# A routed last layer: results scattered to token order inside the block loop

## Chip, cores, metric

The kernel runs on one core of one Trainium2 chip. The metric is the device time of one execution in microseconds.

## What is computed

Sixteen sequences of 256 tokens with 256 features pass through four layers, each with a cross attention and a feed-forward part, added to x through a tanh gate. The change lies in the feed-forward part of the last layer, a mixture of experts (T = 32 tiles of 128 tokens, 32 experts, 4 chosen for each token):

```
logits = flat @ router_w.T + router_bias
scores = softmax(logits); topk_scores, topk_idx = top_k(scores, 4)
topk_scores = topk_scores / clip(topk_scores.sum(), 1e-12)
h = silu(einsum('nd,ehd->neh', flat, gate_w)) * einsum('nd,ehd->neh', flat, up_w)
expert_out = einsum('neh,edh->ned', h, down_w)
sel = take_along_axis(expert_out, topk_idx)          # four rows of 256 for each token
out = (sel * topk_scores).sum(axis=1)
out = out + silu(flat @ sgate_w.T) * (flat @ sup_w.T) @ sdown_w.T
x = x + tanh(g_ffn[3]) * out
```

An expert's hidden width is 128, that of the shared part (the last line but one) 512. All is float32.

## The kernel before

The program is a row of stages, each a block in which five engines run their own instruction lists and meet through semaphores. Stage A (0 to some 2360 us) is the first layer, B the routed part of the second, C all up to the router of the last, D the routed and shared part of the last layer. Everything in D comes from `expert_layer(rd, 128, ..., 0, 1, True)`.

**Cells.** In C, the normed rows of each batch of 256 tokens (tiles `x_e[b % 3]`) are scattered by GpSimd (`scatter_rows`, L1917) into a DRAM tensor `d_cells`. It has a region of 4096 rows for each expert and one more; a row's place is its expert's region plus its rank. Stage A clears the tensor with 66 transfers of 2 MB on SP, five after each batch (L477 to L480). VectorE finds ranks and places in `e_rank` (L2832). The eight scatters of the last batch are the first thing that GpSimd does in D.

**Blocks.** The rows of each expert are cut into blocks of 128; NB = 159 is the fixed number of blocks. A block needs the number of its expert (`block_expert`) and its first cell.

**The order in D.** PE computes the first of eight groups of the shared part: four `shared_in` (L1632, 8 products of 512 columns as the profile counts) and four `shared_out` (L1647), with forty products of the identity between them that nobody reads (L1641 and L1642). Then PE runs the loop over blocks. In round u it transposes the rows of block u+1 (`rows`, L1678), multiplies block u by its gate and up weights (`gate_up`, L1689) and the hidden values of block u-1 by the down weights (`down`, L1701). ScalarE makes silu (L1753), then copies the result of block u-1 out of PSUM (`put_rows`, L1745) and asks for its store to `d_results` in block order (L1747). VectorE copies the transposed rows (L1879) and multiplies the two halves (L1889). GpSimd gathers the rows of block u+4 as soon as buffer u % 4 is free (L1601, an indirect DMA). SP brings the 256 KB of gate and up weights of a block into one of eight buffers (L1569).

**The finish.** After the loop, once all results are stored, GpSimd gathers for each tile of tokens and each of its four choices 128 result rows: 128 indirect DMAs (L1610) into eight buffers, each after the first eight waiting for `added`. VectorE weighs them and adds them to x (`result_add`, L1845), four in each step, between the steps of the shared part of the seven other groups, which PE computes meanwhile; a `shared_add` (L1837) waits until the result adds of earlier tiles are done. SP stores x at the end, batch by batch.

**PSUM.** `ring` has three slots of 1024 columns, `acc` two of 512; a name's slot comes from its place in a written order, and `wait_room`, `wait_full`, `wait_taken` are the waits on them.

## Time and profile before

| | |
|---|---|
| median of 3 runs | 4259.48 us (4255.28 to 4262.33) |
| profiled execution | 4255.14 us |
| its span, first to last instruction | 4253.4 us |
| PE busy | 3971.4 us, 93% |
| VectorE, ScalarE, GpSimd busy | 2250.9, 1746.0, 1066.0 us |
| DMA traffic | 472.83 MB, 111 GB/s over the span |
| layer D | 3759.8 us to the end |
| its loop over blocks | 3791.0 to 4053.8 us |

PE is TensorE's products, PEld its weight loads, DVE VectorE, ACT ScalarE, POOL GpSimd, SP the queue of SyncE. A row of a group gives line, engine, operation, output<-inputs, count, then busy us and mean ns, then the engine's idle time just before, with what ended it. The clock is the share of TensorE's full speed that was granted.

### The profile page before, as it was taken

To read this page: it belongs to the slowest core of one execution; us is meant where nothing else is said; L and a number is where in the kernel's file an instruction comes from. 1 tells how busy PE (TensorE), PEld (TensorE's weight loads), DVE (VectorE), ACT (ScalarE), POOL (GpSimd) and SP (SyncE) were. 2 spreads that over 40 slices of the span, in tenths; PEclk is the share of its full clock that TensorE was granted. 3 is DMA by queue.
4 is the path that set the end of the run, shared out by engine and by line. 5 is a ranking of instruction groups with operands and counts; after the bars stand their busy time and mean duration, and the time that the engine had idled before them with its cause. 6 is when DMAs were issued, how large, how long until landed. Compare 5 with 4: busy or idle time off the path is not lost. (4 is left out here: it accounts for less than half of the span.)

```text
span 4253.4 us, 77426 instructions
## 1 busy us (share of the span) xinstructions
PE 3971.4 (93%) x28880; PEld 2796.9 (66%) x28960; DVE 2250.9 (53%) x6853; ACT 1746.0 (41%) x3685; POOL 1066.0 (25%) x1239
## 2 busy tenths in 40 slices
PE   7999999999999999999998899999998898789987
PEld 4666666666666666666665489976666565468854
DVE  4555665566556555655564521136766665344444
ACT  4445554555455545554542111113544444313310
POOL 2221222122212221222120011111022222245555
PEclk9999999999999999999999999999999898899998
DMA  3003303330333033303310169960212111159934
GB/s 116 2 12 117 116 10 110 117 116 9 110 117 117 11 108 117 117 11 108 115 58 28 75 233 333 334 212 28 66 61 70 60 55 47 43 199 321 322 117 131
DMA packets 285453, 472.83 MB, mean 111 GB/s; under 512 B 23009, under 2 KB 224609, under 8 KB 276513
## 3 DMA queue, kind: packets, MB, share of 16 engines
q1 hardware_dynamic: 227632, 371.88, 25.8%
q0 software_dynamic: 24480, 66.88, 5.1%
q10 hardware_dynamic: 32976, 29.13, 2.0%
q8 instruction: 240, 3.93, 0.4%
q14 instruction: 125, 1.02, 0.1%
HBM read 266.74 MB, written 201.06 MB: 110 GB/s over the span
## 5 line engine op out<-in xcount | busy, mean ns | idle before, releaser
L496 POOL TENSOR_SCALAR a_wide_p<-a_wide_p,a_w_inv 128x512 f32<-128x512 f32 x512 | 356.7, 710 | 1440.3 <-DVE a_w_inv L1164 1440.3
L938 ACT ACTIVATE a_wide_p<-a_wide_p,a_row_min 128x512 f32<-128x512 f32 x512 | 363.6, 713 | 120.5 <-DVE a_row_min L1159 120.3
L1234 DVE TENSOR_REDUCE a_q_pad<-ring 128x4 f32<-128x1024 f32 x256 | 302.3, 1219 | 76.2 <-PE ring L720 76.2
L580 PE MATMUL ring<-a_qk 64*128 64x512 f32 x678 | 288.1, 641 | 19.1 <-ACT a_wide_pt L967 12.2
L1159 DVE CUSTOM_DVE_ANT_0 a_wide_p<-ring,a_neg_keys 128x512 f32<-128x512 f32 x339 | 226.9, 688 | 116.3 <-PE ring L580 115.8
L995 ACT ACTIVATE a_probs<-ring 128x1024 f32<-128x1024 f32 x256 | 251.1, 1022 | 82.1 <-PE ring L734 82.1
L2803 DVE CUSTOM_DVE_ANT_0 shared_w<-ring,c_neg_mask 128x256 f32<-128x256 f32 x512 | 186.4, 421 | 138.8 <-remote 82.2
L1689 PE MATMUL ring<-b_xgt,b_we 128*128 128x128 f32 x2016 | 235.5, 275 | 0.5 <-DVE b_xgt L1879 0.5
L1689 PEld LDWEIGHTS ring<-b_xgt,b_we 128*128 128x128 f32 x2016 | 230.2, 192 | 0.8 <-DVE b_xgt L1879 0.7
L2612 ACT ACTIVATE c_probs<-ring 128x1024 f32<-128x1024 f32 x128 | 131.0, 1024 | 223.5 <-PE ring L2358 176.2
L580 PE MATMUL acc<-a_qk 64*128 64x512 f32 x346 | 194.6, 642 | 8.5 <-ACT a_wide_pt L967 5.0
L598 PE MATMUL ring<-ident,a_wide_p 128*128 128x128 f32 x1376 | 194.9, 277 | 6.8 <-ACT a_wide_pt L967 6.8
L1601 POOL DMA_INDIRECT d_xg<-d_cells,d_token_idx x159 | 150.9, 949 | 122.8 <-PE ring L1678 84.2
L1169 DVE COPY a_wide_pt<-ring 128x512 f32<-128x512 f32 x175 | 118.9, 687 | 110.5 <-PE ring L598 110.1
L598 PEld LDWEIGHTS ring<-ident,a_wide_p 128*128 128x128 f32 x1376 | 152.2, 141 | 35.1 <-issue 14.6
L559 PE MATMUL ring<-a_kv_t,shared_w 128*128 128x512 f32 x352 | 173.0, 614 | 2.2 <-ACT a_kv_t L928 2.2
L2358 PE MATMUL ring<-c_q_t,c_k_t 32*128 32x256 f32 x1024 | 163.7, 440 | 8.7 <-DVE c_q_pad L2803 8.5
L1889 DVE TENSOR_TENSOR b_hid<-b_sil,ring 128x512 f32<-128x512 f32 x63 | 43.4, 689 | 238.3 <-ACT b_sil L1753 238.3
L1689 PE MATMUL ring<-d_xgt,d_we 128*128 128x128 f32 x1272 | 168.2, 275 | 0.5 <-DVE d_xgt L1879 0.5
L734 PE MATMUL ring<-a_q_t,a_k_t 32*128 32x256 f32 x2048 | 147.6, 401 | 21.7 <-ACT a_probs L995 15.0
L588 PE MATMUL ring<-shared_w,a_kv_t 128*128 128x128 f32 x1312 | 163.0, 277 | 1.6 <-ACT a_qk L950 0.4
L588 PEld LDWEIGHTS ring<-shared_w,a_kv_t 128*128 128x128 f32 x1312 | 154.5, 192 | 13.6 <-issue 7.4
(459 smaller groups left out, 8677.1 us busy)
## 6 DMA issues: line engine op xcount, KB each, us to landing
d_cells<-a_neg_keys SPq DMA_DIRECT2D x66, 2048.0 KB, 16.2
b_we<-in_experts SPq DMA_DIRECT2D x63, 1536.0 KB
d_we<-in_experts SPq DMA_DIRECT2D x159, 256.0 KB
d_results<-d_yb ACTq DMA_DIRECT2D x159, 128.0 KB
a_k_t<-in_ctx_keys SPq DMA_DIRECT2D x16, 512.0 KB
a_v_pad<-in_ctx_values SPq DMA_DIRECT2D x16, 512.0 KB
c_k_t<-in_ctx_keys SPq DMA_DIRECT2D x16, 512.0 KB, 3.6
c_v_pad<-in_ctx_values SPq DMA_DIRECT2D x16, 512.0 KB, 3.5
```

The costliest lines, as they stand in the source:

```text
L496: ins = pool.tensor_scalar(wide_p[:, h % 4, t, :], wide_p[:, h % 4, t, :], w_inv[:, t, h:h + 1], 1.0, ALU.mult, ALU.mult)
L559: ins = pe.matmul(wbank(name), wkv[:, c, u * P:(u + 1) * P], kv_t[w % 2][:, c, :], start=(c == 0), stop=(c == C - 1))
L580: pe.matmul(wbank(name), qk[u % 2][64 * j:64 * j + 64, t * P:(t + 1) * P], qk[u % 2][64 * j:64 * j + 64, 256:768], start=True, stop=True). ...
L588: ins = pe.matmul(wbank(name)[:, P * i:P * i + P], kv_t[w % 2][:, c, i * P:(i + 1) * P], wkv[:, c, 1024 + u * P:1024 + (u + 1) * P], start ...
L598: ins = pe.transpose(wbank(name)[:, P * k:P * k + P], wide_p[:, (2 * u + h) % 4, t, k * P:(k + 1) * P], ident[:])
L938: ins = act.activation(wide_p[:, h % 4, t, :], wide_p[:, h % 4, t, :], ACT.Exp, scale=-1.0, bias=row_min[:, h, t:t + 1], accum_out=row_sum ...
L995: act.activation(probs[:, i % 4, :, :, :].rearrange("p j k n -> p (j k n)"), nslot(name), ACT.Exp, scale=HD ** -0.5 if k == "c" else 1.0). ...
L1159: dve.tensor_tensor_reduce(wide_p[:, h % 4, t, :], wbank(name), neg_keys[w % 2][:], -0.125, 3.0e38, ALU.add, ALU.min, row_min[:, h, t:t + ...
L1234: dve.tensor_reduce(q_pad[:, :, 2 * i:2 * i + 2, HD].rearrange("p t h -> p h t"), s, AX.X, ALU.max, negate=True).then_inc(nr.taken(name), 1)
L1689: ins = pe.matmul(ring[:, rg.slot(("gu", u)), UP * j + P * i:UP * j + P * i + P], we[:, u % WB, w0:w0 + P], xgt[:, u % 2, c, :], start=(c ...
L2358: ins = pe.matmul(tbank[:, n:n + 256], k_t[tb % 3][SLOT * r:SLOT * r + SLOT, g, m * P:(m + 1) * P], q_t[SLOT * r:SLOT * r + SLOT, g, :], s ...
L2803: ins = dve.tensor_tensor_reduce(junk[:, 2 * j + t, :], scores[:, j, t, :], neg_mask[:, t, :], -1.0, 3.0e38, ALU.add, ALU.min, q_pad[b % 2 ...
```

## The change

A function `last_layer` takes the place of `expert_layer` for D.

- A row in `d_cells` is 264 numbers long instead of 256 (1056 bytes instead of 1024). The eight more are the token's four chosen experts and the four places that its results have in a DRAM tensor in token order; `e_rank` writes them on VectorE with two operations for each batch. The clearing transfers get longer by the same share. In C some scratch tiles move to other memory.
- In the loop ScalarE asks for the rows of a block, as one plain DMA of 128 consecutive rows, into one of eight buffers: blocks 0 to 7 ahead of the loop, block u+7 in round u behind `put_rows(u-1)`.
- VectorE compares, for four blocks at once, each row's four experts with the block's expert and so gets the place of the result (`find_places`); rows that are only padding get a spare place. It waits for the rows of all four blocks.
- GpSimd scatters the result rows of each block to their places with one indirect DMA, after `find_places` of the block and the copy out of PSUM. The gathers of the loop and the 128 gathers of the finish are gone, and so is the computation of `looked` and `slots` on VectorE.
- In the finish SP fetches the results in token order, one plain DMA of 1 MB for each batch of 256 tokens, six buffers. VectorE adds the eight tiles of a batch in one step, in steps 2 to 17 of 32. SP stores x between the fetches.
- The forty products of the identity are gone. PE reads `block_expert` at the head of a round.
- SP streams the weights block by block as before, with one load of shared tokens moved ahead.

```diff
-cells = nc.dram_tensor("d_cells", ((EXPERTS + 1) * T * P, D), F32, kind="Internal").ap()
+cells = nc.dram_tensor("d_cells", ((EXPERTS + 1) * T * P, D + 8), F32, kind="Internal").ap()
...
-        neg_keys = [sb(ph, f"a_neg_keys{i}", [P, 512]) for i in range(2)]
+        neg_keys = [sb(ph, f"a_neg_keys{i}", [P, 512 + 8 * (1 - i)]) for i in range(2)]
...
-                                     neg_keys[0][:, 256:512].unsqueeze(1).to_broadcast([P, 16, D])).then_inc(cells_cleared, 16)
+                                     neg_keys[0][:, 256:520].unsqueeze(1).to_broadcast([P, 16, D + 8])).then_inc(cells_cleared, 16)
...
-        junk = ws[:, 3072:4096].rearrange("p (s n) -> p s n", s=4)
-        x_e = [last_rows, mask_i[:].bitcast(F32),
-               rb.chosen[:].rearrange("p k t e -> p (k t e)").bitcast(F32).rearrange("p (t d) -> p t d", t=2)]
+        spare = rb.chosen[:].rearrange("p k t e -> p (k t e)").bitcast(F32)
+        junk = [spare[:, 0:256], spare[:, 256:512], ws[:, 3840:4096], sb(ph, "c_junk", [P, 256])[:]]
+        x_e = [last_rows, routed, ws[:, 3072:3072 + 2 * (D + 8)].rearrange("p (t d) -> p t d", t=2)]
...
+                pool.iota(places_of_tokens[:], [[P, 2], [2 * P, 4]], base=rd.NB * P, channel_multiplier=1,
+                          allow_small_or_imprecise_dtypes=True).then_inc(made, 1)
...
+                    dve.tensor_copy(x_e[b % 3][:, :, D:D + 4], rd.choice[:].rearrange("p k t -> p t k"))
+                    dve.tensor_scalar(x_e[b % 3][:, :, D + 4:D + 8], places_of_tokens[:], float(8 * P * b), None, ALU.add)
...
+def last_layer(r, gate, w_experts):
+    K, NB, E, G, HW = r.K, r.NB, EXPERTS, T // 4, P
...
+    cells_of = cells.rearrange("(n p) d -> n p d", p=P)
...
+                sp.dma_start(wd[:], w_experts[:, :, WG:WG + D].rearrange("e p n -> p e n")).then_inc(downs_loaded, 16)
+                def weights(u):
+                    e = sp.value_load(block_expert[u % P:u % P + 1, u // P:u // P + 1], min_val=0, max_val=E - 1)
+                    if u >= WB:
+                        rg.wait_full(sp, ("gu", u - WB))
+                    sp.dma_start(we[:, u % WB, :], w_experts[bass.ds(e, 1), :, 0:WG].rearrange("o p n -> (o p) n")).then_inc(weighted[u % WB], 16)
+                def shared_tokens(u):
+                    rg.wait_full(sp, ("sgu", u - 2, 3))
+                    sp.dma_start(xt[u % 2], r.turned[:, :, 512 * u:512 * u + 512]).then_inc(xt_loaded[u % 2], 16)
+                def fetch(b):
+                    if b >= RES:
+                        sp.wait_ge(added, 2 * K * (b - RES + 1))
+                    sp.dma_start(yk[:, b % RES, :, :], results[NB * P:(NB + K * T) * P, :].rearrange("(b m p) d -> b p m d", m=2 * K, p=P)[b])\
+                      .then_inc(fetched[b % RES], 16)
...
+                sp.wait_ge(experts_ready, 1)
+                for u in range(WB):
+                    weights(u)
+                shared_tokens(2)
+                for u in range(WB, NB):
+                    weights(u)
+                for i in range(YB):
+                    sp.wait_ge(stored[i], 16 * ((NB - 1 - i) // YB + 1))
+                def put_out(b):
+                    sp.wait_ge(added, 2 * K * (b + 1))
+                    ac.wait_taken(sp, ("dn", 2 * b))
+                    ac.wait_taken(sp, ("dn", 2 * b + 1))
+                    sp.dma_start(out.rearrange("b (t p) d -> b p t d", p=P)[b], x_all[:, 2 * b:2 * b + 2, :]).then_inc(out_stored, 16)
+                for b in range(RES):
+                    fetch(b)
+                for n in range(4 * (G - EARLY) + 4):
+                    if n % 4 == 3 and 2 + EARLY + n // 4 < G:
+                        shared_tokens(2 + EARLY + n // 4)
+                    if 2 <= n < B - RES + 2:
+                        fetch(n - 2 + RES)
+                    for b in range(B):
+                        if n == max(b + 2, 2 * b + 5 - 4 * EARLY):
+                            put_out(b)
+                sp.wait_ge(out_stored, 16 * B)
...
+                        scatter_rows(pool, B - 1, t, k, last_rows, scattered)
+                for u in range(NB):
+                    pool.wait_ge(placed, u // 4 + 1)
+                    ac.wait_taken(pool, ("y", u))
+                    pool.indirect_dma_start(out=results, out_offset=bass.IndirectOffsetOnAxis(ap=place[:, u:u + 1], axis=0),
+                                            in_=moved[:, u % YB, :], in_offset=None).then_inc(stored[u % YB], 16)
...
+                def down(u, e):
+                    rg.wait_taken(pe, ("gu", u))
+                    ac.wait_room(pe, ("y", u))
+                    pe.matmul(acc[:, ac.slot(("y", u)), 0:D], hid[:, u % 2, :], wd[:, bass.ds(e, 1), :].rearrange("p o n -> p (o n)"),
+                              start=True, stop=True).then_inc(ac.full(("y", u)), 1)
...
+                        rows(u + 1)
+                    gate_up(u)
+                    if u >= 1:
+                        down(u - 1, before)
+                    before = e
+                down(NB - 1, before)
+                for u in range(EARLY, G):
+                    if u >= 2:
+                        pe.wait_ge(xt_loaded[u % 2], 16 * (u // 2))
+                    for i in range(4):
+                        shared_in(u, i)
+                        if u > EARLY:
...
+                def put_rows(u):
+                    ac.wait_full(act, ("y", u))
+                    if u >= YB:
+                        act.wait_ge(stored[u % YB], 16 * (u // YB))
+                    act.activation(moved[:, u % YB, :], acc[:, ac.slot(("y", u)), 0:D], ACT.Copy).then_inc(ac.taken(("y", u)), 1)
+                def load_rows(u):
+                    row = act.value_load(block_row[u % P:u % P + 1, u // P:u // P + 1], min_val=0, max_val=(E + 1) * T - 1)
+                    if u >= XB:
+                        rg.wait_full(act, ("x", u - XB))
+                        act.wait_ge(placed, (u - XB) // 4 + 1)
+                    act.dma_start(xg[:, u % XB, :], cells_of[bass.ds(row, 1), :, :].rearrange("o p d -> (o p) d")).then_inc(loaded[u % XB], 16)
+                for n in range(4 * EARLY):
+                    shared_silu(n)
+                act.wait_ge(experts_ready, 1)
+                act.wait_ge(scattered, 16 * 2 * K)
+                for u in range(XB):
+                    load_rows(u)
+                for u in range(NB):
+                    rg.wait_full(act, ("gu", u))
+                    if u >= 2:
+                        rg.wait_taken(act, ("gu", u - 2))
+                    act.activation(sil[:, u % 2, :], ring[:, rg.slot(("gu", u)), 0:HW], ACT.Silu).then_inc(silued, 1)
+                    if u >= 1:
+                        put_rows(u - 1)
+                    if XB <= u + 7 < NB:
+                        load_rows(u + 7)
+                put_rows(NB - 1)
+                for n in range(4 * EARLY, 4 * G):
+                    shared_silu(n)
...
+                def find_places(u):
+                    n, s = min(4, NB - u), u % XB
+                    for i in range(n):
+                        dve.wait_ge(loaded[s + i], 16 * (u // XB + 1))
+                    link(dve.tensor_tensor(match[:, 0, 0:n, :], xg[:, s:s + n, D:D + K],
+                                           expert_of[:, u:u + n].unsqueeze(2).to_broadcast([P, n, K]), ALU.is_equal))
+                    link(dve.tensor_tensor(match[:, 1, 0:n, :], match[:, 0, 0:n, :], xg[:, s:s + n, D + K:D + 2 * K], ALU.mult))
+                    link(dve.tensor_reduce(where[:, 0:n], match[:, 1, 0:n, :], AX.X, ALU.add))
+                    dve.tensor_tensor(place[:, u:u + n], where[:, 0:n], spare[:, u:u + n], ALU.max).then_inc(placed, 1)
...
+                def add_results(b):
+                    dve.wait_ge(fetched[b % RES], 16 * (b // RES + 1))
+                    for k in range(K):
+                        for t in range(2):
+                            n = 2 * (K * b + k) + t
+                            if k:
+                                dve.wait_ge(added, n - 1)
+                            dve.scalar_tensor_tensor(out=x_all[:, 2 * b + t, :], in0=yk[:, b % RES, 2 * k + t, :],
+                                                     scalar=shares[:, k, 2 * b + t:2 * b + t + 1], in1=x_all[:, 2 * b + t, :],
+                                                     op0=ALU.mult, op1=ALU.add).then_inc(added, 1)
...
+                rows(0)
+                for u in range(NB):
+                    if u + 1 < NB:
+                        rows(u + 1)
+                    dve.wait_ge(silued, u + 1)
+                    if u >= 2:
+                        ac.wait_full(dve, ("y", u - 2))
+                    dve.tensor_tensor(hid[:, u % 2, :], sil[:, u % 2, :], ring[:, rg.slot(("gu", u)), HW:2 * HW], ALU.mult)\
+                       .then_inc(rg.taken(("gu", u)), 1)
+                    if u % 4 == 1 and u + 3 < NB:
+                        find_places(u + 3)
+                dve.wait_ge(gated, 1)
+                for t in range(4 * EARLY):
+                    ac.wait_taken(dve, ("dn", t))
+                steps = 4 * (G - EARLY)
+                for n in range(steps + 4):
+                    if n < steps:
+                        shared_hidden(4 * EARLY + n)
+                    if n >= 4:
+                        t = 4 * EARLY + n - 4
+                        if n > 2:
+                            dve.wait_ge(added, 2 * K * min(n - 2, B))
+                        shared_add(t)
+                        ac.wait_taken(dve, ("dn", t))
+                    if 2 <= n < B + 2:
+                        add_results(n - 2)
 if "D" in stages:
-    expert_layer(rd, 128, gates[:, 7:8], a["experts3"], 0, 1, True)
+    last_layer(rd, gates[:, 7:8], a["experts3"])
```

## Rows read from the trace of the kernel before

**Rows 1.** Windows of the last layer. Start:end, length, then busy (instructions) by engine, PE clock, DMA.
```profile
3800.00:4040.00 240.00, 235.83 (x1753) 212.69 (x1752) 101.31 (x292) 93.12 (x292) 138.50 (x147) 1.00 0.98 321
...
4082.00:4253.40 171.40, 133.09 (x391) 79.38 (x389) 76.61 (x163) 13.41 (x23) 104.08 (x108) 0.88 0.40 121
```

**Rows 2.** Groups by line and shape, 4053 to 4253 us.
```profile
L1610 POOL DMA_INDIRECT d_yk<-d_results,d_result_slots x128 | 123.2, 962 | 80.4 <-DVE x_all L1845 36.2 <-issue 31.6 <-DMA d_results<-d_yb 12.6
...
L1845 DVE SCALAR_TENSOR_TENSOR x_all<-d_yk,d_gated_shares,x_all 128x256 f32<-128x256 f32 x128 | 57.0, 483 | 28.5 <-DMA d_yk<-d_results,d_result_slots 25.5 <-DVE x_all L1845 1.4 <-issue 0.5
```

**Rows 3.** The chain, 4155 to 4253 us: start, us, what.
```profile
4190.81 1.73 PE acc L1647 x8
4192.54 3.43 PE ring L1632 x8
...
4229.30 0.95 POOL d_yk L1610
4230.25 0.30 issue
```

**Rows 4.** The chain, 3759 to 3792 us.
```profile
3774.26 8.93 PE acc L1642 x80
3783.19 6.92 PE acc L1647 x32
```

**Rows 5.** Timeline of two blocks in the loop: start, us, engine, line, operation.
```profile
3881.72 1.06 PE L1689 MATMUL ring<-d_xgt,d_we 128*128 128x128 f32 x8
...
3882.81 0.28 ACT L1753 ACTIVATE d_sil<-ring 128x128 f32<-128x128 f32 x1 [0.73 <-ACT d_yb L1745]
...
3883.25 0.39 ACT L1745 ACTIVATE d_yb<-acc 128x256 f32<-128x256 f32 x1 [0.16 <-issue]
3883.26 1.06 PE L1689 MATMUL ring<-d_xgt,d_we 128*128 128x128 f32 x8
```

**Rows 6.** Timeline of VectorE in the finish.
```profile
4193.17 1.67 DVE L1845 SCALAR_TENSOR_TENSOR x_all<-d_yk,d_gated_shares,x_all 128x256 f32<-128x256 f32 x4
```

**Rows 7.** The chain, pieces in which a DMA ended a wait.
```profile
3842.25 6.66 DMA d_xg<-d_cells,d_token_idx
...
4054.24 1.70 DMA d_results<-d_yb
...
4075.58 2.50 DMA d_yk<-d_results,d_result_slots
```

**Rows 8.** Timeline of the prelude.
```profile
3774.93 0.69 DVE L1832 TENSOR_TENSOR d_hidden<-d_shared_sil,ring 128x512 f32<-128x512 f32 x1 [2.75 <-ACT d_shared_sil L1736]
3775.08 0.99 POOL L1601 DMA_INDIRECT d_xg<-d_cells,d_token_idx  x1 [4.65 <-DMA d_cells<-last_rows,d_slots]
...
3790.54 0.75 DVE L1879 COPY d_xgt<-ring 128x256 f32<-128x256 f32 x2
...
3791.01 1.16 PE L1689 MATMUL ring<-d_xgt,d_we 128*128 128x128 f32 x8 [0.47 <-DVE d_xgt L1879]
```

**Rows 9.** DMA issues, 200 to 600 us: KB each, median us to landing.
```profile
b_rows<-a_heads SPq DMA_DIRECT2D x2, 256.0 KB, 2.1
```

**Rows 10.** Windows of 4 us at the start of the finish.
```profile
4072.00:4076.00 4.00, 1.40 (x6) 1.27 (x7) 2.46 (x6) 0.26 (x1) 3.08 (x4) 0.98 0.36 103
4076.00:4080.00 4.00, 4.00 (x8) 2.04 (x7) 1.86 (x4) 0.00 (x0) 3.08 (x4) 0.59 0.39 109
```

**Rows 11.** Timeline of VectorE, small operations that wait for one another.
```profile
3748.41 0.17 DVE L2846 TENSOR_TENSOR d_exps<-d_exps,d_sums 128x8 f32<-128x8 f32 x1
3748.61 0.16 DVE L2847 TENSOR_REDUCE d_sums<-d_exps 128x2 f32<-128x8 f32 x1
```

**Rows 12.** Line 1569, SP's queue: duration ns min/median/max.
```profile
L1569 SPq FUSED_REGOPS  x222: 14/42/322, 2423.6 to 4039.1; - x111
```

**Rows 13.** Groups by line and shape, 3800 to 4040 us.
```profile
L1678 PE MATMUL ring<-ident,d_xg 128*128 128x128 f32 x292 | 56.3, 275 | 1.2 <-DMA d_xg<-d_cells,d_token_idx 0.7 <-issue 0.2
```

**Rows 14.** DMA issues of the page.
```profile
c_v_pad<-in_ctx_values SPq DMA_DIRECT2D x16, 512.0 KB, 3.5
```

More of the change, by code:

```diff
@@ L1158, in mask_scores @@
                                 wr.wait_full(dve, name)
-                                dve.tensor_tensor_reduce(wide_p[:, h % 4, t, :], wbank(name), neg_keys[w % 2][:], -0.125, 3.0e38,
+                                dve.tensor_tensor_reduce(wide_p[:, h % 4, t, :], wbank(name), neg_keys[w % 2][:, 0:512], -0.125, 3.0e38,
                                                          ALU.add, ALU.min, row_min[:, h, t:t + 1]).then_inc(wr.taken(name), 1)
@@ L1912, in build @@
         rd = Routing(top, "d", 4, True)
-        last_rows = sb(top, "last_rows", [P, 2, D])
+        last_rows = sb(top, "last_rows", [P, 2, D + 8])
         def scatter_rows(pool, b, t, k, rows, scattered):
@@ L1952, in build @@
                 w3 = sb(ph, "c_w3", [P, C, D])
-                mask_i = sb(ph, "c_mask_i", [P, 2, 256], I32)
+                routed = sb(ph, "c_routed", [P, 2, D + 8])
+                mask_i = routed[:].rearrange("p t d -> p (t d)")[:, 0:512].bitcast(I32).rearrange("p (t k) -> p t k", t=2)
+                places_of_tokens = sb(ph, "c_places_of_tokens", [P, 2, 4])
                 neg_mask = sb(ph, "c_neg_mask", [P, 2, 256])
@@ L2057, in build @@
                     loads = [
-                        (mask_i[:], a["mask_qk"].rearrange("(t p) k -> p t k", p=P)),
+                        (mask_i, a["mask_qk"].rearrange("(t p) k -> p t k", p=P)),
                         (win[:], a["win_twice"].rearrange("(c p) n -> p c n", p=P)),
@@ L2802, in n_maxima @@
                                 for t in range(2):
-                                    ins = dve.tensor_tensor_reduce(junk[:, 2 * j + t, :], scores[:, j, t, :], neg_mask[:, t, :], -1.0, 3.0e38,
+                                    ins = dve.tensor_tensor_reduce(junk[2 * j + t], scores[:, j, t, :], neg_mask[:, t, :], -1.0, 3.0e38,
                                                                    ALU.add, ALU.min, q_pad[b % 2][:, t, 2 * s + j, HD:HD + 1])
@@ L2825, in e_apply @@
                                 dve.wait_ge(e_scattered[b % 3], 16 * 2 * rd.K * (b // 3))
-                            norm_give(rd.norm, e_given, b, lambda t: x_e[b % 3][:, t, :]).then_inc(e_ready, 1)
+                            norm_give(rd.norm, e_given, b, lambda t: x_e[b % 3][:, t, 0:D]).then_inc(e_ready, 1)
                         def e_count_taken(b):
@@ L2888, in mask_in @@
                             dve.wait_ge(loaded, 16 * len(loads))
-                            dve.tensor_scalar(neg_mask[:], mask_i[:], 0.0, -BIG, ALU.is_equal, ALU.mult).then_inc(masked, 1)
+                            dve.tensor_scalar(neg_mask[:], mask_i, 0.0, -BIG, ALU.is_equal, ALU.mult).then_inc(masked, 1)
                         def mask_turned():
@@ L2904, in _ @@
                             if i == -1:
-                                dve.wait_ge(made, 2)
+                                dve.wait_ge(made, 3)
                             if on(x2):
```

200 lines of the change are left out of this document (added).

## The prediction

> **What bounds the kernel now.** I read the windows first. The changed layer is the last 493.6 us of 4253.4: a prelude from 3759.8 to 3791.0, the loop over 159 blocks to 4053.8, and the finish. In the loop PE is busy 98% of the time and the DMA engines move 321 GB/s at a share of 0.98: both are near their limit. In the finish PE has 133 of 171 us and the DMA share is 0.40, so neither is [rows 1].
>
> The groups by line say what the finish waits for [rows 2]: 128 gathers on POOL, 0.96 us each with some 0.30 of issue between them, behind `added`, and VectorE idle for their landing. The chain shows it as 0.95 of gather and 0.30 of issue again and again, and PE going only now and then at its own pace of 3.43 us for a `shared_in` and 1.73 for a `shared_out` [rows 3].
>
> The chain of the prelude is all PE: 16+16 `shared_in`, the forty dummy products (8.93 us), `shared_out` (6.92), then the first rows [rows 4]. The timeline of the loop gives one block [rows 5]: gate_up at 3881.72 and again at 3883.26, a period of 1.54 us. Ideal 159 x 1.545 = 246 us; it took 262.8 (3791.0 to 4053.8), 1.65 a block.
>
> **Finish.** Gone are the 128 gathers and the wait for slots. PE then has 28 x (3.43 + 1.73) = 144.5 us [rows 3]. Is another engine slower? VectorE per step of 5.16 us: one hidden product 0.69 [rows 8], one shared add 0.5 and now eight result adds (two tiles by four), which run at 1.67 us for four when nothing is missing [rows 6]: 0.69 + 0.5 + 3.3 = 4.5 us, under 5.16, so the wait `added` stays behind PE. Fetches are 16 x 1 MB and with the stores of x some 23 MB in 145 us, 155 GB/s, half of what the loop moves. The first: last result taken 0.4 us after the loop, scatter issued by 1.7, landed 2.5 later like a gather [rows 7] (4.7 as after the prelude's scatters [rows 8]), 1 MB in some 5.5 more: it is there 9.7 to 12 us after the loop, and its adds end at 13 to 15.5. PE has five `shared_in` (17.2 us) before it needs a hidden product queued behind those adds. That covers the fetch; without it each us late would be a us. `shared_tokens(3)` on SP is now behind `fetch(6)`, which waits for the adds of batch 0: about 15 us after the loop, needed only at 35. After the last product: an add 0.5, the store of x 2.1 (a 256 KB store [rows 9]), 0.4 of waits. I take 150 us with 2.5 for the odd gap, against 199.6: **-49.6** (bounds -52 with no gap, -35 if the adds or fetches hold PE back by a tenth).
>
> **Prelude.** The dummies go, but `shared_out` needs the fourth hidden product (3774.93 + 0.69 [rows 8]), so it starts at 3775.8 and ends at 3782.7. Then the fourth shared add, `find_places(0)` (0.8, below), the copy of rows(0), and 0.47 to gate_up as before (3790.54 to 3791.01 [rows 8]): 3784.4, **-6.6**. The rows are asked for at 3775.1, when the scatters landed [rows 8]; even 6.7 us of landing [rows 7] would not delay this by one. Bounds 0 and -8.9. Clock: PE now stands idle 1.5 us there. The clock showed 0.59 after 4 us in which PE was busy for 1.40 only [rows 10]; a gap of 1.5 I take as free. The 10 us of `looked` work on VectorE were hidden and give nothing.
>
> **Loop.** Taken out: POOL's gather (a load from ACT instead) and ACT's store (a scatter from POOL instead). Bytes per block 512 KB before, 516 now. POOL still has one issue of 1.25 us a block. ACT has 0.28 + 0.38, a value load and an issue of 0.33 as before: near 1.3 of 1.54. PE's value load goes ahead of the transposes; PE's queue has the down product in hand there and I take nothing.
>
> What is new is VectorE's wait. `find_places(u+3)` sits in its order after hid(u) for u = 5, 9, ..., 153 (38 times that can stall), and waits for the rows of blocks u+3 to u+6. Block u+6 is asked for by ACT in its round u-1, after `put_rows(u-2)`: one round earlier only. Everything of VectorE is queued behind it: rows(u+2), without which PE has no gate_up(u+2), so ACT asks for no rows either. Follow one cycle from F, the start of the copy that comes after a find. gate_up F+0.47; the next gate_up 1.55 later, F+2.02; its silu 1.09 later and the copy of y 0.44 behind that (3882.81, 3883.25 [rows 5]), F+3.55; a value load, and the request goes out at F+3.85. It lands L later; the find is four small operations 0.20 apart [rows 11], 0.8. **Cycle of four blocks = 4.65 + L**, where an undisturbed one is 6.2 and the present mean 6.6.
>
> The value load on ACT is not in the trace: SP's register operations take 0.04 in the middle, 0.32 at most [rows 12]; I take 0.3, bounds 0.04 to 0.6. L, for 132 KB: a 128 KB store landed 1.70 after its issue when the DMAs were idle, gathers in the finish 2.50 and, now and then, one in the loop 6.66 [rows 7]. Most gathers of the loop landed inside the three blocks that four buffers give, under 4.3 us, since PE's transposes idled only 1.2 us in all there [rows 13]. A 512 KB load takes 3.5 at light load [rows 14]; less 380 KB at 340 GB/s that is 2.4. In the new cycle the DMAs carry 2.06 MB, 6.4 us of work in some 7.4, beside a weight transfer (0.8 us) and a scatter (0.4): I add 0.4, **L = 2.8**, bounds 1.7 and 4.3.
>
> The Trainium skill (DMA: Bandwidth & Descriptors, Anatomy of one DMA) gives a DMA a fixed 2.0 us and its bytes at 436 GB/s: an estimate of 2.3 us for these rows, by which the sum below would be -41 instead of -22. The rows at light load agree with it.
>
> Cycle 7.45. 38 x 7.45 + 7 other blocks at 1.65 = 294.7, against 262.8: **+31.9**. Each us of L is worth 38 us. Bounds: L of 2.0 or less meets the DMAs' own 6.45 a cycle, about +1.5; L = 4.3 gives +89.
>
> **Stages before.** e_rank gets two VectorE operations a batch, 0.17 each: 5.6 us over 16 batches, in a stage where neither engine sets the pace alone. I take 2, bounds 0 and 5.6, and 0.4 for the last batch, which is on the way to the barrier. Clearing `cells` moves 3% more, waited for by nobody before the stage's end, and stage A's loads stand ahead of each burst of five: 0. Junk tiles, mask view, iota: 0.
>
> **Sum.** -49.6 - 6.6 + 31.9 + 2.4 = -21.9 on an execution of 4255.1. The median of the runs is 4.3 above it: 4259.5 - 21.9 = **4238 us**.
>
> **Rivals.** (1) The wait costs nothing: ScalarE's sequencer runs ahead and rows land in 2.0 to 2.3 us. For it: the 1.70 store. Against: that store was alone. Then the loop is at +1 to +13 and the time is 4207 to 4219. 0.13.
> (2) The other side, slower: the same wait, with loaded rows landing like those of the present loop. From L = 3.6 on it decides: 38 x (4.65 + L) takes more than finish and prelude give. For it: the 6.66 [rows 7], and a DMA share that stays over 0.8. At L = 3.9 it is +20, 4280; at 4.3 +35, 4295, and PE then idles 2.5 us a cycle, not far from what goes before the fallen clock of [rows 10]. Against: a stalled cycle asks for less, so queues empty. 0.18.
> The Trainium skill (the same page, Latency and other measured facts) gives HBM 0.2 us on average and 2 at high load. Put on the 2.3 above, that is an estimate of L = 4.1 and +27: rival 2. No row tells how much of the loop's landing is this.
> (3) Between, within 0.2% (8.5 us, about what these runs can tell): L from 3.15 to 3.6, or the finish gives a third less. 0.14.
> (4) My own case, L from 2.3 to 3.15, 4219 to 4251: 0.55.
>
> **Numbers.** Faster is (1) and (4), 0.68; same 0.14; slower 0.18. Range 4207 to 4280: L from 2.0 to 3.9, which leaves out half of (2) and the corner below. The likeliest case has 4219 to 4251.
>
> **What would show it.** In the profile after: VectorE idle before the first `match` operation of every fourth block, ended by the DMA of `d_xg`, 1.0 to 1.5 us each; PE idle of the same size before gate_up two blocks on; loop 280 to 308 us. Finish near 150 us with PE over 95% and clock 1.0, no POOL work. First gate_up some 25 us after the layer's first product. I am wrong if that VectorE wait is absent, or above 2.5 us; or if PE in the finish waits for hidden products behind `fetched`.

## The result: 4338.6 us, slower by 1.85%

| | before | changed |
|---|---|---|
| median of 3 runs | 4259.48 us | 4338.57 us (4332.07 to 4341.14) |
| ratio | | 1.0185, 95% interval 1.0167 to 1.0204 |
| layer D begins | 3759.8 | 3764.1 |
| its prelude | 31.2 | 26.3 |
| its loop over 159 blocks | 262.2 | 397.2 |
| its finish | 200.2 | 149.3 |
| span | 4253.4 | 4336.9 |

I had forecast 4238, range 4207 to 4280. The differences of the four stretches, +4.3 - 4.9 + 135.0 - 50.9 (the loop is taken here from the first gate_up to the start of the last down product), make the 83.5 us of the spans. Three of them are near the forecast (+2.4, -6.6, -49.6); the loop is not (+31.9).

The windows of the changed kernel, to be read beside [rows 1]: start:end, length, busy (instructions) of PE, PEld, DVE, ACT, POOL, then clock, DMA share, GB/s.

```profile
3764.10:3790.40 26.30, 21.99 (x74) 12.90 (x74) 9.26 (x32) 3.59 (x5) 8.25 (x12) 1.00 0.98 342
3790.40:4187.60 397.20, 301.04 (x1903) 268.94 (x1903) 128.61 (x473) 103.38 (x317) 150.17 (x157) 0.87 0.67 204
4187.60:4336.90 149.30, 145.25 (x450) 85.33 (x450) 84.44 (x184) 17.10 (x29) 2.28 (x3) 0.99 0.50 161
```

PE does the same 301 us of work in 397 us, and the DMA engines fall from 0.98 to a share of 0.67. Neither is the limit any more. The waits of the loop name what is:

```profile
DVE d_match L3286 <- DMA d_xg<-d_cells: 95.9, 35, 4.3
...
PE ring L3165 <- DVE d_xgt L3320: 74.8, 26, 4.1
```

VectorE stood in `find_places` for the DMA of `d_xg` 35 times, 95.9 us in all, and PE's gate_up stood behind VectorE's copy. This is the wait of the prediction, in its place, though longer: 2.7 us each in the mean and up to 4.3, above the 2.5 that I had named as a sign of being wrong. The chain through one cycle shows its size (start, us, what):

```profile
3947.32 4.26 DMA d_xg<-d_cells
...
3951.70 0.18 DVE d_match L3286
...
3952.40 0.43 DVE d_xgt L3320
...
3952.97 2.04 PE ring L3165 x8
...
3956.29 0.98 PE ring L3165 x8
...
3957.73 0.29 ACT d_chosen L3218
...
3958.04 0.15 ACTq L3221
...
3958.47 4.16 DMA d_xg<-d_cells
```

From F (3952.40, the copy after a find) to the next request for rows (3958.47) it is 6.07 us, where I had 3.85; the rows land after 4.26 and 4.16, where I had 2.8; the find takes 0.7. And gate_up, 0.89 long at full clock, takes 2.04.

The landing that a find waits for can be read for each of the 37 finds that waited: from the issue of its youngest rows on ScalarE's queue to its first `match` operation, less the 0.12 us between landing and operation that the chain shows. It is 3.75 us in the mean, from 2.05 to 5.25. F to the request is 5.63 in the mean, from 4.45 to 7.26. With the 0.8 of a find they make the mean cycle of 10.20 us. One short landing, issue and operation:

```profile
3939.92 0.34 ACTq L3225 DMA_DIRECT2D d_xg<-d_cells  x1
...
3942.09 0.18 DVE L3286 TENSOR_TENSOR d_match<-d_xg,b_so_far 128x16 f32<-128x16 f32 x1 [1.09 <-DMA d_xg<-d_cells]
```

The windows of this landing and of the next one, which took 4.26:

```profile
3939.92:3941.97 2.05, 2.05 (x18) 1.93 (x17) 0.31 (x2) 0.66 (x2) 0.96 (x1) 1.00 0.77 188
3947.32:3951.58 4.26, 2.53 (x19) 2.09 (x18) 0.29 (x1) 1.21 (x4) 2.59 (x3) 1.00 0.88 276
```

The same holds all through this loop: the nine landings under 2.8 us met a DMA share of 0.64 to 0.78, the other 28 one of 0.81 to 0.96. Windows of 2 us around another wait show the clock:

```profile
3828.00:3830.00 2.00, 2.00 (x17) 1.77 (x15) 0.29 (x1) 0.94 (x3) 1.33 (x2) 1.00 0.87 254
3830.00:3832.00 2.00, 0.21 (x2) 0.00 (x0) 0.90 (x5) 0.38 (x1) 1.41 (x2) 1.00 1.02 361
3832.00:3834.00 2.00, 1.73 (x11) 1.54 (x12) 0.91 (x4) 0.28 (x1) 0.13 (x1) 0.86 0.75 261
3834.00:3836.00 2.00, 2.00 (x11) 2.00 (x10) 0.46 (x2) 0.38 (x1) 0.74 (x1) 0.50 0.54 140
3836.00:3838.00 2.00, 2.00 (x15) 1.72 (x14) 0.71 (x2) 0.66 (x2) 0.22 (x1) 0.79 0.67 167
3838.00:3840.00 2.00, 2.00 (x17) 1.79 (x16) 0.29 (x1) 0.85 (x3) 1.21 (x2) 1.00 0.78 229
```

PE is busy 0.21 of 2 us, then the clock is 0.86, 0.50, 0.79 of full speed: at its lower level, 1.2 GHz, in all of the middle one of these three windows and in a part of the other two, just when PE has work again. And while VectorE waits for its rows, the DMA engines are at a share of 1.02 and move 361 GB/s: the mean of 0.67 hides that the transfers come in bunches.

In the finish nothing is left of the gathers. PE is busy 145.3 of 149.3 us at a clock of 0.99; VectorE's result adds have 0.5 us of idle time before them in all. The fetches took 10.0 us to land, being asked for six at a time, and held nobody.

### The profile page after: what moved, and what is told of

Read it like the earlier page. It is cut to its first block and busy times, and to the rows that moved or that the text cites. A ratio compares the mean times of both kernels' runs of the same rounds, so it can differ in the third digit from the quotient of the medians.

```text
span 4336.9 us, 78447 instructions
## 1 busy us (share of the span) xinstructions
PE 3999.7 (92%) x28800; PEld 2822.1 (65%) x28880; DVE 2259.2 (52%) x7036; ACT 1747.9 (40%) x3685; POOL 941.9 (22%) x1112
## 5 line engine op out<-in xcount | busy, mean ns | idle before, releaser
L3165 PE MATMUL ring<-d_xgt,d_we 128*128 128x128 f32 x1272 | 199.8, 308 | 97.6 <-DVE d_xgt L3320 77.6
L995 ACT ACTIVATE a_probs<-ring 128x1024 f32<-128x1024 f32 x256 | 251.1, 1022 | 82.4 <-PE ring L734 82.4
L3165 PEld LDWEIGHTS ring<-d_xgt,d_we 128*128 128x128 f32 x1272 | 182.6, 221 | 105.6 <-DVE d_xgt L3320 83.3
L3113 POOL DMA_INDIRECT d_placed_results<-d_chosen,d_place x159 | 152.4, 959 | 263.4 <-ACT d_chosen L3218 178.9
L2807 DVE CUSTOM_DVE_ANT_0 b_chosen<-ring,c_neg_mask 128x256 f32<-128x256 f32 x256 | 98.2, 421 | 143.7 <-remote 83.8
## 6 DMA issues: line engine op xcount, KB each, us to landing
d_cells<-a_neg_keys SPq DMA_DIRECT2D x66, 2112.0 KB, 18.8
```

The costliest lines, as they stand in the source:

```text
L995: act.activation(probs[:, i % 4, :, :, :].rearrange("p j k n -> p (j k n)"), nslot(name), ACT.Exp, scale=HD ** -0.5 if k == "c" else 1.0). ...
L3165: ins = pe.matmul(ring[:, rg.slot(("gu", u)), HW * j:HW * j + P], we[:, u % WB, w0:w0 + P], xgt[:, u % 2, c, :], start=(c == 0), stop=(c = ...
```

## The experiments

They ran on three other chips, which were quicker: the kernel before took 4095 to 4102 us there. Ratios are always to the kernel before on the same chip, and stretches are compared by stretch.

**1. Find the places later (e1).** Only VectorE's order changes.

```diff
-                            if u % 4 == 1 and u + 3 < NB:
-                                find_places(u + 3)
+                            if u % 4 == 3 and u + 1 < NB:
+                                find_places(u + 1)
```

> One edit to the changed kernel: find_places(u+1) at u = 3, 7, 11, ... in place of find_places(u+3) at u = 1, 5, 9, ..., so that the youngest rows it waits for were asked for four rounds before its own round, not one. My theory (the loop is long because VectorE waits for rows asked for one round earlier, and the clock falls behind that wait): the 96 us of waiting for d_xg before the first match operation go to under 10, the clock in the loop is back at 1.0, the loop takes 262 to 280 us in place of 398, and the time is 4200 to 4220. Rival (the new transfers themselves, rows of 1056 bytes and scattered stores, are too slow for the loop): the loop stays above 300 us with PE waiting for DMAs in another place, and the time above 4240.

(The youngest rows are asked for three rounds earlier, not four as I wrote.) Measured: 4072.35 us against 4094.71, ratio 0.9945 (0.9933 to 0.9957). The loop's window, and what is left of the wait:

```profile
3669.40:3926.30 256.90, 252.99 (x1903) 226.26 (x1904) 129.27 (x473) 101.67 (x317) 149.73 (x157) 1.00 0.95 315
```

```profile
DVE d_match L3286 <- DMA d_xg<-d_cells: 5.3, 13, 0.8
```

The loop takes 256.9 us, with every new transfer in it: rows of 1056 bytes, scattered stores, requests from ScalarE. PE's clock is 1.00 and the DMA share 0.95. So the transfers are not too slow for the loop, and the rival falls. The time itself is below my 4200 to 4220 because I had the other chip's other stages in mind; the loop is a little below my 262 to 280, too. It is still 6 us longer than the loop of the kernel before on such a chip (251.1, experiment 5), so what the change gains here, 0.6%, comes from prelude and finish.

**2. Keep PE busy in the gap (e2).** The clock by itself.

```diff
                             for c in range(C):
+                              for _ in range(13 if u and u % 4 == 0 else 1):
                                 ins = pe.transpose(ring[:, rg.slot(("x", u)), c * P:(c + 1) * P], xg[...], ident[:])
```

> The changed kernel with PE kept busy in the gap: the two transposes of every fourth block (the ones ahead of the stalled gate_up) are made 13 times instead of once, 24 more products, about 2.6 us, with the same result. If the fallen clock is a cost of its own: the clock in the loop returns to near 1.0, the gate_up behind the wait takes 0.89 to 1.1 us instead of 2.04, a cycle of four blocks 8.6 to 9.0 us instead of 10.1, and the time is 4275 to 4300. Rival (the wait alone sets the cycle, the clock is only its sign): 4330 to 4345. The landing of the rows stays at 4.2 to 4.5 us in both.

Measured: 4200.79 us, ratio 1.0250 (1.0236 to 1.0265), against 1.0277 of the changed kernel (experiment 6). The chain of a cycle, and the loop's window:

```profile
3824.38 0.43 DVE d_xgt L3321
...
3824.94 1.13 PE ring L3166 x8
...
3826.73 0.89 PE ring L3166 x8
...
3828.84 4.63 DMA d_xg<-d_cells
```

```profile
3671.00:4054.10 383.10, 357.12 (x2839) 331.32 (x2840) 128.02 (x473) 103.57 (x317) 149.60 (x157) 1.00 0.68 212
```

The clock is 1.00, gate_up after the wait takes 1.13 us, and the request comes 4.46 us after F (4.56 in the mean, against 5.72 in experiment 6). Yet the loop only falls from 396 to 383 us, a cycle from 10.2 to 9.8. The landing is 4.63 us in this cycle and 4.45 in the mean, against 3.65, and VectorE's wait has grown from 103 to 132 us. So the clock costs some 12 us of the kernel's time where I expected 38 to 63: of the 1.16 us a cycle that it gives back, 0.80 are spent again in the landing. That the transfers are the slower because they are asked for in a shorter time fits the shares above; no run shows it by itself.

**3. Rows that start on multiples of 256 bytes (e3).** `d_cells` gets rows of D + 64 numbers, of which D + 8 are cleared and loaded; the scatters still write D + 8.

```diff
-cells = nc.dram_tensor("d_cells", (..., D + 8), ...)
+cells = nc.dram_tensor("d_cells", (..., D + 64), ...)
...
-cells_of[bass.ds(row, 1), :, :]
+cells_of[bass.ds(row, 1), :, 0:D + 8]
```

> The changed kernel with rows of d_cells 1280 bytes apart instead of 1056, so that each starts on a multiple of 256; the bytes moved are the same. If crooked starts make the transfers slow: the clearing transfers land in 16.5 to 17 us instead of 18.8, the rows in under 4.0 instead of 4.3, and the time falls by 10 us or more. Rival (the landing is latency and sharing): rows still 4.2 to 4.5, the time within 8 us of 4338.

Measured: 4211.67 us, ratio 1.0278 (1.0264 to 1.0293), that of the changed kernel. The issues of the clearing (0 to 2300 us) and of the rows, KB each and median us to landing:

```profile
d_cells<-a_neg_keys SPq DMA_DIRECT2D x66, 2112.0 KB, 18.9
```

```profile
d_xg<-d_cells ACTq DMA_DIRECT2D x159, 132.0 KB, 4.3
```

The median of the rows goes over a part of the 159 loads only, those whose landings the profile can tell. The same view of the changed kernel as it is (experiment 6) has other loads in it, and another median:

```profile
d_xg<-d_cells ACTq DMA_DIRECT2D x159, 132.0 KB, 2.2
```

So these two medians cannot be compared; what can be is the landing that the finds wait for, 3.79 us in the mean here and 3.65 in experiment 6, and the loop, 399.1 and 396.1. Nothing moved. Where the rows start is not what makes them late. The Trainium skill (DMA: Bandwidth & Descriptors, How a descriptor splits into AXI transactions) has a descriptor that starts off a multiple of 256 bytes cost extra beats on the bus; neither the clearing nor the loads show it here.

**4. No weights in the loop (e4).** SP loads the weights of blocks 0 to 7 only, and the later blocks use what lies in the buffers, so the routed part is computed with the weights of other experts.

```diff
-                        for u in range(WB, NB):
-                            weights(u)
...
-                            pe.wait_ge(weighted[u % WB], 16 * (u // WB + 1))
+                            pe.wait_ge(weighted[u % WB], 16)
```

> The changed kernel without the gate and up weights of blocks 8 to 158: those blocks use what lies in the eight buffers, so half of the loop's bytes are not moved. If rows land late because they share the DMA engines with the weights: 2.4 to 3.0 us instead of 4.3, a cycle near 7.5, the time 4220 to 4270. Rival (the landing has its length by itself): still 4 us or more, the time above 4310.

Measured: 4121.27 us, one run. Its chain, and the issue of the rows:

```profile
3825.37 0.43 DVE d_xgt L3318
...
3829.83 2.10 DMA d_xg<-d_cells
```

```profile
d_xg<-d_cells ACTq DMA_DIRECT2D x159, 132.0 KB, 2.1
```

With nothing else changed in the order, the awaited rows land in 2.3 us in the mean (median 2.1) instead of 3.7, and the loop takes 300.5 us instead of 396, a cycle 7.7. F to the request is again 4.46. The time is 91 us below the changed kernel's of experiment 6, inside the 68 to 118 that I expected. The waits are shorter, too, and PE's clock stays up (0.99 in the loop). So with the clock up the company of the weight transfers makes up half of the landing: 2.1 of the 4.45 us of experiment 2.

The Trainium skill (DMA: Bandwidth & Descriptors, Anatomy of one DMA) gives its fixed cost for DMAs that GpSimd issues; these are ScalarE's. The estimate of 2.3 us that I made with it is near what this run shows without the weights, at a DMA share of 0.46. With the weights it does not hold.

**5 and 6. Both kernels on one chip (e5, e6).**

> The kernel before, unchanged, for a profile from the chip of this call. On the chip of the first experiments it took 4095 us, on the first one 4259 us, and PE's clock in the stage before the last layer was 0.98 there and 0.91 here. If the finish gains from the clock too: its 200 us are 160 to 170, close to 128 gathers of 1.25 us. Rival: the finish is 195 to 205 us on every chip and only the stage before it differs.

> The changed kernel, unchanged. Both theories have its loop at 395 to 400 us and its finish at 149. If the finish of the kernel before is shorter on this chip, the ratio is worse than 1.0185: 1.027 to 1.030. If not, 1.018 to 1.021.

Measured: 4101.80 (one run) and 4212.63 us, the latter 1.0277 (1.0260 to 1.0294) of the kernel before. Prelude, loop and finish of the kernel before on this chip, then the loop of the changed one:

```profile
3643.80:3677.40 33.60, 33.12 (x154) 22.90 (x154) 18.29 (x36) 3.64 (x5) 12.51 (x17) 0.93 0.67 235
3677.40:3928.50 251.10, 247.92 (x1903) 228.71 (x1904) 112.57 (x318) 104.59 (x317) 145.59 (x155) 1.00 0.98 325
3928.50:4100.10 171.60, 150.28 (x450) 87.66 (x450) 91.09 (x184) 17.10 (x29) 123.76 (x128) 0.94 0.46 140
```

```profile
3666.00:4062.10 396.10, 301.22 (x1903) 269.28 (x1904) 128.19 (x473) 103.72 (x317) 150.47 (x157) 0.86 0.67 205
```

The kernel before has a finish of 171.6 us here and 200.2 on the first chip, and its loop is 251.1 instead of 262.2. The changed kernel has 396.1 and 149.1, as on the first. So the new finish gives 51 us on one chip and 22.5 on the other, and the change costs 79 us there and 113 here. Of the 28.6 us by which the old finish is longer on the first chip, most stands before its gathers, which wait for result adds; first that chip, then this one:

```profile
POOL d_yk L1610 <- DVE x_all L1845: 36.2, 25, 5.7
```

```profile
POOL d_yk L1610 <- DVE x_all L1845: 8.5, 28, 0.3
```

PE's clock in this finish is 0.89 there and 0.94 here; whether it is the cause isn't shown. With the order of experiment 1 I would expect a larger gain on the first chip than the 0.6% measured on these; that wasn't run there.

**7. Two rounds ahead (e7).**

```diff
-                            if u % 4 == 1 and u + 3 < NB:
-                                find_places(u + 3)
+                            if u % 4 == 2 and u + 2 < NB:
+                                find_places(u + 2)
```

> The changed kernel with find_places(u+2) at u = 2, 6, 10, ...: the youngest rows it waits for were asked for two rounds earlier instead of one. If the wait is a plain race between the landing and the rounds in between, one more round of 1.55 us shortens every cycle by at least that, by more where the clock stays up: a cycle of 7.9 to 8.5 us, a loop of 310 to 340 us. Rival (something else in a find holds the loop up): a loop of 380 us or more.

Measured: 4121.65 us, ratio 1.0059 (1.0042 to 1.0076). The loop's window and the wait of this kernel:

```profile
3667.10:3967.90 300.80, 257.85 (x1903) 229.58 (x1904) 127.85 (x473) 102.40 (x317) 150.19 (x157) 0.99 0.86 269
```

```profile
DVE d_match L3286 <- DMA d_xg<-d_cells: 49.6, 37, 2.3
```

The wait halves, from 102.6 us in experiment 6 to 49.6, the clock is back at 0.99, and the loop is 300.8 us, a little better than my 310 to 340; a cycle is 7.6, where I had 7.9 to 8.5. One, two and three rounds ahead give 396, 301 and 257: a race between the landing and the rounds in between, and nothing else in a find.

**8. Experiment 1 beside them (e8).**

> The kernel of the first experiment again, beside the kernel before and the changed one on one chip: loop 255 to 262 us, finish 149, and 128 to 145 us below the changed kernel.

Measured: 4074.53 us, ratio 0.9941 (0.9923 to 0.9958), 138 us below the changed kernel; loop 257.2, finish 149.1.

**9 and 10. Rows of 1024 bytes (e9, e10).** Experiment 9 is experiment 1 again, to compare with. Experiment 10 has `d_cells` of D numbers in all its transfers. It leaves out the transport of the chosen experts and places: the match takes the last eight features in their stead, at the same size, and finds nothing, so every result goes to a spare place, and these are counted out over the region that is fetched. What the routed part adds is therefore not the reference's.

```diff
-cells = nc.dram_tensor("d_cells", (..., D + 8), ...)
+cells = nc.dram_tensor("d_cells", (..., D), ...)
...
-in_=rows[:, t, :]
+in_=rows[:, t, 0:D]
...
-pool.iota(spare, [[P, NB]], base=0, ...)
+pool.iota(spare[:, 0:P], [[P, P]], base=NB * P, ...)
+pool.iota(spare[:, P:NB], [[P, NB - P]], base=0, ...)
...
-act.dma_start(xg[:, u % XB, :], ...)
+act.dma_start(xg[:, u % XB, 0:D], ...)
...
-xg[:, s:s + n, D:D + K]
+xg[:, s:s + n, D - 2 * K:D - K]
-xg[:, s:s + n, D + K:D + 2 * K]
+xg[:, s:s + n, D - K:D]
```

> The kernel of the first experiment once more, as what the two others of this call are compared with: prelude 27.5 us, loop 257, finish 149, clearing transfers 18.9 us to land.

> The first experiment's kernel with rows of 1024 bytes in d_cells, in their clearing, scattering and loading. The chosen experts and places are left out of the rows; find_places reads the last eight features instead and every row goes to a place counted by block and lane, so the results are not those of the reference, while every operation has its old size. If the odd 32 bytes at the end of a row cost something of their own: the clearing transfers land in 16.2 us instead of 18.9, and the loop takes 251 to 254 us instead of 257. Rival (only 3% more bytes): clearing 18.3 or more, the loop unchanged within 2 us.

Measured: 4070.51 us, ratio 0.9938 (0.9925 to 0.9952), and 4076.04 us, 0.9952 (0.9936 to 0.9967). The issues of the clearing (x count, KB each, median us to landing), of experiment 9 and then of 10:

```profile
d_cells<-a_neg_keys SPq DMA_DIRECT2D x66, 2112.0 KB, 18.9
```

```profile
d_cells<-a_neg_keys SPq DMA_DIRECT2D x66, 2048.0 KB, 16.5
```

The clearing lands in 16.5 us instead of 18.9: 3% more bytes took 15% longer. The loop is 258.1 us with the long rows and 259.5 with the short ones, so the 32 bytes cost the loop nothing; I had expected 251 to 254. Nor does the clearing's time reach the end: nobody waits for it.

**11. Two shared groups ahead of the loop (e11).** Experiment 1 with EARLY = 2, `shared_tokens(3)` behind `shared_tokens(2)`, and the second group's products between those of the first on PE and VectorE.

```diff
-WG, WB, XB, YB, EARLY, RES = 2 * C * HW, 8, 8, 8, 1, 6
+WG, WB, XB, YB, EARLY, RES = 2 * C * HW, 8, 8, 8, 2, 6
...
+shared_tokens(3)
...
+    shared_in(1, i)
+    shared_out(i)
+for i in range(4, 8):
...
+    shared_hidden(4 + n)
+    shared_add(n)
+for n in range(4, 8):
```

> The first experiment's kernel with two of the eight groups of the shared part ahead of the loop instead of one. PE stands idle for some 5 us there while the last rows are scattered and loaded, and the second group has 20.7 us of products. If PE's idle time can be used: the prelude grows by 13 to 16 us, the finish shrinks by 20.7 to 128.4, and the time is 4 to 8 us lower. Rival (the group is only moved, the start of the loop waits for all of it): 0 to 2 us.

Measured: 4068.56 us, ratio 0.9933 (0.9919 to 0.9946). The windows of its prelude and finish:

```profile
3637.90:3683.70 45.80, 44.65 (x137) 25.90 (x137) 13.84 (x40) 5.97 (x9) 8.25 (x12) 0.95 0.62 208
...
3941.60:4070.10 128.50, 124.50 (x386) 73.05 (x386) 79.75 (x176) 14.74 (x25) 2.27 (x3) 1.00 0.56 183
```

The finish shrinks by 20.6 us to 128.5, but the prelude grows by 18.3 to 45.8: 2 us below experiment 9, less than the two intervals can tell apart. PE's idle time in experiment 9 was 3 us, not the 5 that I had written, and this uses 2 of them. The rival holds. This and experiment 1 beat both kernels, each by an interval clear of 1.

## Why the prediction was wrong

**The finish** was right: 150 forecast, 149.3 measured, PE as the limit, no wait for fetches. What I did not see is that the 199.6 us it is measured against belonged to the first chip: on another they are 171.6.

**The prelude** came to 26.3 us where I had 24.6. The scatters of the last batch landed as long after D began as before, 15.3 us. What I left out is that `find_places(0)` needs the rows of four blocks and that ScalarE asks for them one behind the other: the first request's value load starts at 3779.51, the fourth request goes out 4.1 us later, and its rows take 5.3 to land. So gate_up waited for rows and not, as I had it, for the fourth shared add:

```profile
3773.73 5.70 DMA d_cells<-last_rows,d_slots
...
3779.51 0.48 ACTq L3221
...
3783.59 5.32 DMA d_xg<-d_cells
```

**The stages before**: +4.3 against +2.4 on the first chip; between profiles of variants of the changed kernel on one chip the start of D differs by more (3634.0 in experiment 3, 3643.5 in experiment 2), so neither number is confirmed.

**The loop** is the step that failed: "Cycle of four blocks = 4.65 + L" with "L = 2.8". Its mechanism, the wait of VectorE for rows asked for one round before, its 38 times and its place in the chain were right; moving the find (experiments 1 and 7) takes the wait away and with it all but some 6 us of the loss. Wrong were the sizes in the cycle. Means in us, to which a find adds 0.8:

| | F to the request | landing L | cycle |
|---|---|---|---|
| forecast | 3.85 | 2.8 | 7.45 |
| changed kernel | 5.63 | 3.75 | 10.20 |
| the same, experiment 6 | 5.72 | 3.65 | 10.20 |
| clock held up (2) | 4.56 | 4.45 | 9.83 |
| without weights (4) | 4.53 | 2.30 | 7.66 |

The 103 us that were missing are 38 times the differences of the first two rows, within 1 or 2 us:

- The clock, 38 x 1.17 = 44 us, which the forecast put at nothing. F to the request is 4.46 at full clock and 5.63 in the mean. I took a gap of 1.5 us as free, and that was so: after each of the ten waits of 1.0 to 1.8 us it was 4.75 at most. But the waits were 2.7 us in the mean, and after 21 of the 26 waits of 1.9 us or more it was 5.8 or longer.
- The landing, 38 x 0.95 = 36 us. I had weighed the DMA's mean load and added half a weight transfer. But behind a wait the blocks follow in a bunch, and their weights, stores and rows with them, so the DMA engines are near full while most of the rows are awaited. Whether the company costs queueing in the engines or time in memory, no run tells apart.
- F to the request at full clock, 4.46 instead of 3.85: 38 x 0.61 = 23 us. Some 0.4 of it is the value load on ScalarE, which takes (min/median/max, ns)

```profile
L3221 ACTq TENSOR_LOAD <-d_block_row x159: 275/287/627, 3779.5 to 4174.9; - x159
L3221 ACTq FUSED_REGOPS  x159: 152/152/167, 3780.0 to 4175.3; - x159
```

together 0.44 and with the short instructions behind them 0.74 from the start of the copy to the request; I had taken 0.3 from SP's register operations, whose row did not hold the load itself. The rest is the slower first gate_up after a gap, 1.13 for 0.89, and gaps between steps.

44 + 36 + 23 = 103, and 31.9 + 103 = 135. These terms are not independent. The slow PE delays the request, and meanwhile transfers drain (the window of clock 0.50 above has a DMA share of 0.54): the rows of each of the seven requests that went out 7.0 us or more after F landed in 2.6 us or less. With the clock held up the loop is only 13 us shorter, and then the landing is the larger part, 63 us over the forecast against 27.

Rival 2, the other side, is what happened, and from the point it named (L from 3.6 on). But with L = 3.75 alone the forecast's own formula gives 4274 us, inside the range; what took the time out of it is the other term, F to the request, of which rival 2 mentioned only a gap "not far from" the fallen clock and gave it no price. So the range, cut at L = 3.9, ended 59 us too low. The Trainium skill's figure for memory at high load (DMA: Bandwidth & Descriptors, Latency and other measured facts) had given an estimate of L = 4.1, between the 3.75 of the changed kernel and the 4.45 of experiment 2; I gave it to the less likely case.

## What to carry to other kernels

Where an in-order engine waits for a transfer, count the rounds between the request and the wait, and price the wait with the landing under the load that the wait itself bunches, not under the mean. A check on data brought by a prefetch undoes the prefetch unless it looks only at the old ones: here two lines moved by two rounds are worth 3.3%. A gap on PE should be priced with the clock that follows it, but keeping the clock up is worth less than that price while the wait is for a transfer, since an earlier request met a longer landing here. And a gain that is measured against a finish with gaps should be expected to differ from chip to chip.

## What the hardware showed

- The same kernel took 4259 us on one chip and 4095 to 4102 us on three others. Up to 2300 us the traces of the first chip and of experiment 5 run alike, with 16,688 and 16,687 products and clocks of 0.99 and 1.00. The difference comes behind that: 116 us up to D, 11 in the loop (262.2 and 251.1, at a clock of 1.00 in both) and 29 in the finish. From 3200 to 3400 us the clock was 0.86 on the first chip and 1.00 on the other. What made the loop differ, and whether the gaps or the clock came first elsewhere, isn't shown. The windows of the kernel before, on the first chip and in experiment 5 (the clock is the figure before the last two):

```profile
3200.00:3400.00 200.00, 176.01 (x1392) 118.60 (x1413) 127.77 (x551) 83.68 (x156) 50.11 (x55) 0.86 0.22 68
```

```profile
3200.00:3400.00 200.00, 196.28 (x1752) 137.90 (x1776) 162.19 (x698) 103.54 (x195) 64.22 (x69) 1.00 0.27 84
```

- A row of 1056 bytes in place of 1024 lengthened the clearing's landing by 15 to 16% (16.2 to 18.8, 16.5 to 18.9), wherever it started.
- A plain load of 132 KB that VectorE waited for landed in 2.3 us (mean) with a DMA share of 0.46 in its loop, and in 3.75 with 0.67. Within that second loop it took 2.05 to 2.75 us where the share while it was under way was 0.64 to 0.78, and 3.0 to 5.25 where it was 0.81 to 0.96.
